# A decoder layer's first attention: the transposed causal products replaced by a GpSimd select, with another order of steps

## The reference, cut to what matters

```python
attn = jnp.einsum('bhqd,bhkd->bhqk', q, k) * scale
causal = jnp.tril(jnp.ones((T, T), dtype=bool))
attn = jnp.where(causal, attn, -jnp.inf)
attn = jax.nn.softmax(attn, axis=-1)
y = jnp.einsum('bhqk,bhkd->bhqd', attn, v)
```

## Time and profile before

| | |
|---|---|
| runs | 5859.25, 5866.38 (median), 5866.96 us |
| the profiled execution | 5857.93 us, its span 5856.2 us |
| busy over the span | TensorE 94%, VectorE 74%, ScalarE 56%, GpSimd 35% |
| part A | from about 157 to 1184 us |

### The profile page before, as it was taken

How to read it: one execution, slowest core, us unless ns; L and a number is a source line. 1 busy time by engine, 2 the same in 40 slices (tenths; PEclk the granted TensorE clock), 3 DMA queues, 4 the chain that set the end, 5 groups by cost and what they waited for, 6 DMA issues and landing times. The chain is left out here.

```text
span 5856.2 us, 150644 instructions
## 1 busy us (share of the span) xinstructions
PE 5507.3 (94%) x45977; PEld 4313.5 (74%) x45977; DVE 4335.1 (74%) x11737; ACT 3283.8 (56%) x7315; POOL 2037.6 (35%) x1753
## 2 busy tenths in 40 slices
PE   0999999979999999799999999977899999999998
PEld 0677777757777777567777777753788888888887
DVE  7889898868888888588888888879555555455554
ACT  4788888746666666477777777747223232232322
POOL 0222222223333333234444444430334343333433
PEclk9999999989999999899999999998999999999999
DMA  5777777646666666466676767642322222222221
GB/s 154 180 181 182 183 184 182 169 135 175 173 173 175 174 173 175 115 166 181 168 181 169 179 170 180 170 113 2 71 54 41 52 50 39 51 48 41 55 38 24
DMA packets 625563, 750.63 MB, mean 128 GB/s; under 512 B 131075, under 2 KB 554188, under 8 KB 625328
## 3 DMA queue, kind: packets, MB, share of 16 engines
q1 hardware_dynamic: 568992, 679.62, 44.3%
q0 software_dynamic: 49152, 63.10, 6.7%
q10 hardware_dynamic: 7184, 5.00, 0.4%
HBM read 476.49 MB, written 272.24 MB: 128 GB/s over the span
## 5 line engine op out<-in xcount | busy, mean ns | idle before, releaser
L1489 PE MATMUL exp_res<-exp_w,exp_hT 128*128 128x256 f32 x4096 | 926.0, 380 | 0.0
L1489 PEld LDWEIGHTS exp_res<-exp_w,exp_hT 128*128 128x128 f32 x4096 | 769.8, 190 | 97.9
L1682 POOL DMA_INDIRECT out_dram<-exp_gated,exp_token x256 | 406.2, 1587 | 990.8 <-issue 357.0
L931 DVE TENSOR_REDUCE F_tops<-F_score 128x2 f32<-128x512 f32 x1024 | 684.4, 687 | 60.8 <-PE F_score L685 41.1
L822 ACT ACTIVATE F_probs<-F_scoreT 128x512 f32<-128x512 f32 x1024 | 583.7, 590 | 235.8 <-PE F_scoreT L654 235.8
L931 DVE TENSOR_REDUCE A_tops<-A_score 128x3 f32<-128x384 f32 x1024 | 531.6, 554 | 63.7 <-PE A_score L671 55.5
L1545 ACT ACTIVATE exp_lone<-exp_lead 128x256 f32<-128x256 f32 x256 | 98.3, 384 | 766.5 <-PE exp_lead L1499 747.9
L822 ACT ACTIVATE A_probs<-A_scoreT 128x384 f32<-128x384 f32 x1024 | 451.2, 488 | 23.5 <-PE A_scoreT L642 14.9
L1539 ACT ACTIVATE exp_hT<-exp_hT,exp_b 128x512 f32<-128x512 f32 x512 | 339.3, 712 | 92.6 <-DVE exp_hT L1625 92.6
L654 PE MATMUL F_scoreT<-QS,KS 98*128 98x256 bf16 x2048 | 365.3, 275 | 9.6 <-ACT F_probs L822 1.5
L685 PE MATMUL F_score<-KS,QS 96*128 96x256 bf16 x2048 | 363.4, 275 | 8.7 <-DMA KS<-d_k 7.8
(11 more groups left out here) (357 smaller groups left out, 14519.1 us busy)
## 6 DMA issues: line engine op xcount, KB each, us to landing
QS<-d_q SPq DMA_DIRECT2D x384, 192.0 KB, 3.6
KS<-d_k SPq DMA_DIRECT2D x256, 192.0 KB, 4.0
QS<-d_q SPq DMA_DIRECT2D x384, 128.0 KB, 3.9
KS<-d_k SPq DMA_DIRECT2D x256, 128.0 KB, 4.0
d_q<-A_q_parts SPq DMA_DIRECT2D x64, 384.0 KB, 3.5
d_k<-A_k_parts SPq DMA_DIRECT2D x64, 384.0 KB, 3.8
QS<-d_q SPq DMA_DIRECT2D x384, 64.0 KB, 3.6
d_q<-X_q_parts SPq DMA_DIRECT2D x64, 384.0 KB, 3.9
```

The lines of the kernel that those rows point to most:

```text
L931: nc.vector.tensor_reduce(dst, src, AX.X, ALU.max).then_inc(score_read, 1)
L1489: last = mm(res[t][:, s, :], hT[par][:, f, (2 * t + s) * P:(2 * t + s + 1) * P], w2[k][:, f, :], start=begin and f == fs[0], stop=f == BY_ ...
L1682: nc.gpsimd.indirect_dma_start(out, bass.IndirectOffsetOnAxis(token[j % (2 * XB)][:, s:s + 1], 0), gated[par][:, s, :], None, bounds_check ...
```

## The change

The two causal products of `attend` go. GpSimd gets four steps `cut0` to `cut3`. Each waits for the four exponentials of a group and then sets what lies above the diagonal to zero, by a select over the first 256 of the 384 columns of each of four heads, 1024 elements on every partition, in place. `pv` waits for the cut instead of for the exponentials. `cut3` belongs to the batch before, as `pv3` does. The mask on the side of `maxima` stays. The lists of part A are in another order on all five engines, and `k_store` belongs to a batch one nearer than before.

```diff
     "A": {
-        "SP": ("rowsB fetch loadA rowsA tok1 loadB q_store k_store"),
-        "PE": ("v attend pv3 maxima attend maxima maxima rowsB attend attend tok0 maxima maxima attend xT attend "
-              "maxima tok1 q pv0 attend maxima k maxima attend attend maxima maxima attend pv1 maxima rowsA "
-              "maxima attend attend maxima attend attend pv2 attend maxima attend maxima maxima"),
-        "ACT": ("evac3 attend attend rowsB attend attend xT attend attend q attend evac0 attend k attend attend "
-              "evac1 attend attend rowsA attend attend q_rest evac2 k_rest attend attend"),
-        "DVE": ("topB v maxima maxima maxima tok0 maxima maxima maxima tok1 maxima maxima maxima topA maxima "
+        "SP": ("rowsB fetch k_store loadA tok1 rowsA loadB q_store"),
+        "PE": ("v attend pv3 maxima attend maxima maxima rowsB tok0 attend attend maxima xT maxima attend maxima "
+              "attend q tok1 attend maxima attend maxima maxima k maxima attend pv0 attend maxima pv1 rowsA "
+              "maxima attend attend maxima attend attend attend maxima attend pv2 maxima maxima"),
+        "ACT": ("evac3 attend attend rowsB attend attend xT attend attend q attend attend k evac0 attend evac1 "
+              "attend attend attend rowsA attend k_rest attend attend q_rest attend evac2"),
+        "DVE": ("topB v maxima maxima maxima tok0 maxima maxima maxima tok1 maxima maxima maxima maxima topA "
               "maxima norm maxima maxima maxima maxima maxima"),
-        "POOL": ("q k q_rest k_rest"),
+        "POOL": ("cut3 cut0 cut1 q k cut2 k_rest q_rest"),
...
-SHIFTED = {"A": {},
+SHIFTED = {"A": {"k_store": 2},
...
                             if kind == "A":
-                                for n in range(2):
-                                    mm(s[:, n * P:(n + 1) * P], C["causal"][:, 0:P], ident_b[:, :], start=n == 0,
-                                       stop=False, skip_group_check=True)
-                                mm(s[:, 0:P], k[0:98, i, P:256], q[0:98, i, P:256], start=False, stop=False,
-                                   skip_group_check=True)
-                                last = mm(s[:, P:384], k[0:98, i, 0:P], q[0:98, i, :], start=False, stop=True,
-                                          skip_group_check=True)
+                                mm(s[:, 0:P], k[0:98, i, P:256], q[0:98, i, P:256], start=True, stop=True)
+                                last = mm(s[:, P:384], k[0:98, i, 0:P], q[0:98, i, :], start=True, stop=True)
...
-                            pe.wait_ge(probs_full, G * g + (m + 1) * 4 // HB)
+                            if kind == "A":
+                                pe.wait_ge(probs_cut, 4 * g + m + 1)
+                            else:
+                                pe.wait_ge(probs_full, G * g + (m + 1) * 4 // HB)
...
+                        if name[:3] == "cut":
+                            m = int(name[3])
+                            hold(pool, probs_full, G * g + 4 * m + 4, C["passed"])
+                            diagonal = probs[m % 2][:, :, 0:256].rearrange("p u (n x) -> p u n x", n=2)
+                            nc.gpsimd.affine_select(out=diagonal, in_=diagonal, compare_op=ALU.is_ge, fill=0.0, base=0,
+                                                    pattern=[[0, 4], [0, 2], [1, P]], channel_multiplier=-1)\
+                                .then_inc(probs_cut, 1)
```

More of the change, by code:

```diff
@@ L395, in attention @@
            "attend": 0, "pv0": 0, "pv1": 0, "pv2": 0, "evac0": 0, "evac1": 0, "evac2": 0,
-           "pv3": -1, "evac3": -1, "refetch": -1, "tok0": -1, "tok1": -1, "aT": -1, "proj": -1,
+           "cut0": 0, "cut1": 0, "cut2": 0, "cut3": -1, "pv3": -1, "evac3": -1, "refetch": -1, "tok0": -1, "tok1": -1, "aT": -1, "proj": -1,
            "ustats": -1, "uaggr": -1, "uvar": -1, "uapply": -1, "h2T": -2, "route": -2,
@@ L495, in attention @@
             absmax, best, best_all = sb("absmax", [P, 1]), sb("best", [P, 1]), sb("best_all", [P, 1])
-            reduced = sem("reduced")
+            reduced, probs_cut = sem("reduced"), sem("probs_cut")
         if kind == "X":
```

## The result

The changed kernel took **6043.81 us**, the median of 4 runs (6040.64 to 6047.32); the kernel before took 5865.18 beside it. The ratio is 1.0307, 95% interval 1.0289 to 1.0324: 180 us slower. The profiled execution took 6047.32 us, its span is 6045.6.

The account below looks back on a forecast made before the run. TensorE was taken to bound part A at 15.81 us a turn; with the cuts a turn was 18.85, so 3.04 us times 64 = 195 us on 5857.9 gave 6053, stated as 6055 us, range 5885 to 6115.

Parts of the forecast that it names:

- What bounds part A: Before the change: TensorE bounds part A, 15.81 us a turn over 64 turns, ScalarE 2.5 us behind, VectorE closer.
- What is removed: Causal products on TensorE: 0.12 us per attend, 123 us over 64 turns, a gain only if no other engine holds the turn.
- What a cut costs: GpSimd's select over 1024 elements: 1.3 us, between 1.03 and 2.31.
- The end of a batch: Exponential 15 to evac3: q_rest, cut3 and pv3 make the gap 3.24 us, against 1.27 before.
- The middle of a batch: From pv3's start S: GpSimd blocks topA, exponential 10 starts S + 12.75, exponential 15 ends S + 16.5, next pv3 S + 18.85.
- `norm` "ends some 2 us late ... so it adds nothing": VectorE's norm beside cut2 and k_rest: last maxima delayed to S + 18.5, still ahead of next pv3, adding nothing.
- The moves: Reordered steps: SyncE's moves cost nothing; ScalarE's and VectorE's moves were counted within the walk through the turn.
- The sum: Part A: 3.04 us more a turn, times 64 = 195 us, giving 6053 and a stated 6055 us.
- Rival 1: VectorE's topA gets through in one piece or ahead of cut1: turn 17.1 us, 5941 us; chance 0.27.
- Rival 2: End of batch: cut3 is hidden and removed products pay, VectorE holding about 14.5 us a turn, 5774 us; chance 0.17.
- Rival 3: Select costs 2.3 us, in cut1 and cut3: 20.9 us a turn, 6183 us, TensorE's clock may fall; chance 0.11.
- Its list of what would show it: Expected signs: turn near 18.9 us, select near 1.3, ScalarE idle about 3 before evac3, TensorE near 75% busy.

Follow-up runs that it names:

- r2_old_order: All four cuts and no causal products, but the step lists of the kernel before, with the cuts set between GpSimd's steps: 6103.99 us, ratio 1.0418.
- r12_old_selects_aside: Kernel before, products and order kept, plus four GpSimd selects on a spare tile nobody reads, pv waiting for the exponentials: 6041.05 us, ratio 1.0300.
- r3_no_cut: Changed kernel without its cuts, pv waiting for the exponentials, causal products still gone: 5938.82 us, ratio 1.0139.
- r9_old_order_cut0: Kernel before in its own order with one cut: heads 0 to 3 lose their products, cut0 first in GpSimd's list: 5840.38 us, ratio 0.9959.
- r4_cut3_first: Changed kernel with cut3 moved ahead of q_rest, into its own batch: 5985.53 us, ratio 1.0214.
- r5_hold_q: Changed kernel with one wait more: GpSimd's q waits until VectorE has done topA: 6009.18 us, ratio 1.0250.
- r6_cut3_hold: Changed kernel with cut3 ahead of q_rest and GpSimd's q waiting for topA, both together: 5986.67 us, ratio 1.0210.
- r8_three_cuts_hold: Changed kernel with q waiting for topA, heads 12 to 15 taking causal products again and cut3 gone: 5961.22 us, ratio 1.0166.
- r1_order: Kernel before with only the new order of steps on all engines, causal products kept and nothing cut: 5981.82 us, ratio 1.0207.
- r10_old_order_cut01: r9_old_order_cut0 plus a second cut, cut1, for heads 4 to 7, with pv1 and evac1 later: 5874.21 us, ratio 1.0020.
- r13_new_selects_aside: r1_order plus the changed kernel's four selects at their places, on a spare tile nobody reads: 6030.64 us, ratio 1.0284.

## Why the prediction was right, step by step

The median was forecast at 6055 and came at 6044, by the mechanism that I named. But two terms of the turn missed in opposite directions, so that part of the closeness is luck, and the experiments show a part of the loss that the working never separated. TensorE's clock, which costs the changed kernel some 8 us and r2_old_order some 75, is in none of the terms.

- **What bounds part A.** Right, for the kernel before: r12_old_selects_aside holds TensorE up for 2.5 us a turn, and the turn is 2.7 us longer (176 / 64).
- **What is removed.** The 0.12 us for an `attend` is right: `attend` at 907.66 in the changed kernel is followed by `maxima` at 907.83, 0.17 instead of 0.28. "A gain only as far as no other engine holds the turn" is right too: 40 of 123 us in r3_no_cut, 24 of 31 in r9_old_order_cut0.
- **What a cut costs.** Forecast 1.3 us between 1.03 and 2.31. Alone it takes 1.10 us, and 1.30 where `norm` is beside it; the mean over the kernel is 1.146. The memset's slope on the select at 128 elements, my lower bound of 1.03, was the better estimate. The Trainium skill, GPSIMD Engine Reference, Elementwise — side-by-side cycle accounting, with 1.8 cycles an element would give an estimated 1.54 us; the trace does not agree with that figure, 1.10 us for 1024 elements are 1.3 cycles at its 1.2 GHz.
- **The end of a batch.** Forecast gap 3.24, measured 3.91 and 3.56 in alternation. The chain `q_rest`, `cut3`, `pv3` is right. `q_rest` ended 1.25 after exponential 15 and not 0.91, since `cut2` and `k_rest` before it took 1.30 and 1.32 beside `norm`; then came 0.50 us of pause, which the sum did not have; `cut3` took 1.11 instead of 1.3, and the two handovers 0.02 more: 0.34 + 0.50 - 0.19 + 0.02 = **+0.67**. In the other kind of turn the pause is 0.25 and the miss +0.32. r4_cut3_first shows that the chain holds, and that its price is well under the length of the gap.
- **The middle of a batch.** Forecast exponential 6 at S + 6.67, exponential 10 at S + 12.75, exponential 15 ending at S + 16.5; measured, with S = 906.59, S + 6.78, S + 12.29, and (ScalarE, 922.52) S + 15.93: **-0.6**. The rule "one operation of VectorE at each seam" is right: `topA` asked at S + 9.08 (forecast 8.9), two of its steps were held, and it ended at S + 11.38 (forecast 11.75), as GpSimd's operations start 1.07 and 1.11 apart and not 1.3 and 1.2. The first of these is the mis-sized select again. What held `topA` were the two subtractions; that a select does the same, for which the prediction had no row, r12_old_selects_aside shows (`cut2` and L959), and `cut2` beside `norm` in the changed kernel.
- **`norm` "ends some 2 us late ... so it adds nothing".** In the changed kernel only its last step is held (1.20 instead of 0.43), so it does add nothing. As a statement on what is late next it failed: once `topA` is freed, all of `norm` is blocked, and that takes most of the gain away (r5_hold_q, r6_cut3_hold). r6_cut3_hold was expected too fast for that reason and for the clock, r8_three_cuts_hold also because its theory forgot the order.
- **The moves.** This is what the prediction lacks. It walked the new order with the cuts in it and never asked what it costs by itself. It costs 121 us, about half of it, by the timeline, through `pv2` behind the last `attend`, and most of the rest through TensorE's wait for a reduction behind `k`. With the cuts in, `pv2` is hidden in the gap that `cut3` makes, so the sum was not hurt; but the 195 us of the sum are not what the cut costs. SyncE's moves were called free; no run has them alone.
- **The sum.** From `pv3` to `pv3`, as I had counted, the turn that I followed took 18.56 us (906.59 to 925.15) and its neighbours 18.84; the forecast was 18.85, the mean at full clock 18.70. The turns alternate as GpSimd's pause ahead of `cut3` does (0.50 and 0.25); that this is the whole cause is not shown, since r1_order alternates without a select. Four of 51 turns in the middle of part A take 20.4, each with a stretch at 1.2 GHz (the one from 830 us for example), which lifts the mean to 18.82. The turn before, 15.81 by the exponential that I had picked, is 15.88 by `xT`. Times 64, 18.82 - 15.88 gives 188, and between the two profiled executions the difference is 189 (6047.3 less 5857.9); the medians differ by 179. So the 195 are 6 too many against the profiled execution. The last line slipped as well: 6053 and the 8 between median and profiled execution are 6061, not 6055; from 6061 the miss is 17 us, from 6055 11.
- **The rivals.** Rival 1 did not come: two of three steps were held. r5_hold_q makes it come artificially, and it is worth 33 us, not 114. Rival 2 needed a gap and idle time below 2.78 us; ScalarE idles 3.53 and 3.19 in the gap alone. r9_old_order_cut0 is its true core: with one cut, in idle time, the removed products do pay. Rival 3 fell with the select's 1.10 us. Its side remark on the clock came true in a small way: 0.99 over 200 to 1100 us in the changed kernel, and 0.92 in r2_old_order.
- **Its list of what would show it.** The turn 18.9 (18.56 and 18.84), TensorE about 75% (79), the select within 1.0 to 1.6, two of L940 to L942 blocked at a time, parts X and F unchanged: these came. "Idle about 3 us" was 3.53.

**r2_old_order beside r12_old_selects_aside.** The first lies 69 us above the second (245 less 176), though its VectorE loses less (1.9 us a turn above its unblocked means, against 3.5). TensorE's clock accounts for it: at full clock the turns of r2_old_order take 18.61 to 18.88 us, no longer than those of r12_old_selects_aside (18.76 to 19.01), but the first has a stretch at 1.2 GHz in 43 of 51 turns and the second in 3. Over all 51 the means are 19.92 and 18.97.

**Still open:** why the clock falls so often in r2_old_order and seldom in the changed kernel, where TensorE is as little busy (80% of 200 to 1100 us in both); how the order's 121 us divide, which only the timeline tells; what holds the turn of r8_three_cuts_hold; and the 31 us of r10_old_order_cut01. An order of steps made anew around the blocked operations was not tried.

## What to carry to other kernels

An engine that is 29% busy is not free if it shares a path with a busy one: before work goes to GpSimd, find VectorE's short chained operations that another engine waits for, and put GpSimd's work where none of them lies. A change that comes with a new order of steps is two changes; run the order alone first. When a block at one place is removed, look at what the blocking engine does instead: here the same 3 us of VectorE moved from `topA` to `norm`, and two edits that gave 55 and 33 us alone gave 57 together. And before a difference between two runs is put down to a wait, compare TensorE's granted clock over the whole stage, not in one slice: here 69 us between two runs were the clock.

## What the runs showed of the hardware that I had not expected

- GpSimd's hold on VectorE's operations costs 176 us with nobody waiting for a select (r12_old_selects_aside), at a GpSimd 48% busy in part A. It takes one-input operations too: a cast of 128x16 (mean 175 to 840 ns) and the scalings of `norm` (427 to 1201 or more), but never `maxima`'s reductions (five in 2.46 us beside GpSimd, in 2.52 before). The Trainium skill, SBUF — State Buffer, Who interferes with whom, has it that casts and scalings can be held, that operations with two inputs in SBUF are, and that reductions never are; the traces agree.
- It works in the other direction as well. Beside `norm` a select takes 1.30 us instead of 1.10 and `k_rest` 1.32 instead of 1.16. The Trainium skill, SBUF — State Buffer, Who interferes with whom, also says that who comes first holds the pair for the whole instruction; the trace agrees, since `norm`'s L953 (900.93) runs when `cut2` begins (901.01).
- GpSimd's pause between the last subtraction and `cut3` can be read as a sum. Where the next operation follows a wait of GpSimd on itself and no more, it is 0.08 us (`k_rest` to `q_rest`), and 0.07 for `cut3` in the written-out turns at the start, outside the loop (190.96). Inside the loop the wait of a select is followed by an increment of a semaphore: 0.25 (also `k_rest` to `cut3` in r4_cut3_first). With two such waits it is 0.41 (r13_new_selects_aside). The loop's body holds two batches, and every second time its branch comes on top: 0.50, and 0.68 with two waits. So the wait costs an estimated 0.17 us and the branch 0.25 (differences of these).
- TensorE's clock falls to 1.2 GHz in short stretches in some of the kernels in which TensorE waits. Before the one at 830 us in the changed kernel it had waited 1.74 us for `cut3`, and `pv3` then took 1.49 us instead of 0.86. A turn that holds such a stretch takes 20.4 us instead of 18.56 or 18.84 in the changed kernel (4 of 7 such turns; the other 3 are no longer than usual), 18.7 instead of 17.19 in r3_no_cut, and 0.4 us more than the others in r4_cut3_first. The kernel before and r9_old_order_cut0, with TensorE 99.8% busy, have no such turn in the middle of part A, but r1_order, r8_three_cuts_hold and r13_new_selects_aside, at 87 to 92%, have none either.
- A select over 128 x 1024 float32 takes 1.10 us, 1.07 ns an element; from the 288 ns at 128 elements to there the slope is 0.91 ns an element (the small one was bfloat16).
